# Another table of run lengths for two merged streams, memory of its own for the expert biases' parts, and a wait between head divisions, in a kernel of two transformer layers

## The reference

```
x = x + cross_attention(layernorm(x), ctx, mask)      # 16 heads of 8; 77 context rows, some masked
h = layernorm(x)
y = h + self_attention(layernorm(h) * g1 + c1)        # 16 heads of 8; 512 x 512 scores
z = layernorm(y) * g2 + c2
y = y + expert[argmax(z @ gate_w + gate_b)](z)        # 8 experts: 128 -> 512 (relu) -> 128, each with biases b1, b2
x = x + y
x = x + cross_attention(layernorm(x), ctx)            # scores minus slope * distance
h = layernorm(x)
x = x + h + sigmoid(h @ w_router) * ffn(h) for the 256 tokens of the highest score, x + h for the rest
                                                      # ffn: 128 -> 512 (gelu) -> 128
```

## Time and profile before

| what | value |
|---|---|
| median of three timed runs | 732.77 us (731.79 to 733.81) |
| profiled execution, from first to last instruction | 729.7 us (no time of its own beside the span is given) |
| PE busy | 658.3 us, 90% |
| VectorE busy | 399.1 us, 55% |
| ScalarE busy | 295.5 us, 40% |
| POOL busy | 73.0 us, 10% |
| mean granted clock of PE | 0.963 of 2.4 GHz |

### The profile page before, as it was taken

One profiled execution on the slowest core, in us unless ns is written; L12 is line 12 of the kernel. 1 busy time (PEld: TensorE's weight loads), 2 busy tenths in 40 slices (PEclk: granted clock), 3 DMA queues, 4 the chain that ended last, 5 costly groups with the idle time before them and its releaser, 6 DMA issues.

```text
span 729.7 us, 12018 instructions
## 1 busy us (share of the span) xinstructions
PE 658.3 (90%) x4584; PEld 373.8 (51%) x4588; DVE 399.1 (55%) x924; ACT 295.5 (40%) x354; POOL 73.0 (10%) x82
## 2 busy tenths in 40 slices
PE   3887899999999988899887899999999999999885
PEld 2643434333458645688534453344334388895553
DVE  3635747754852234464716984788348414143657
ACT  1131256356443343242243314645665532314243
POOL 4406401000100001001101100100001000101000
PEclk9997999999999999899998899999999999999998
DMA  8120000000140001310000100000000222200000
GB/s 251 33 91 0 1 1 1 1 1 0 42 129 17 1 2 40 102 45 16 1 1 1 29 1 1 1 1 1 1 1 1 73 73 86 76 2 1 1 1 29
DMA packets 16486, 21.07 MB, mean 29 GB/s; under 512 B 4210, under 2 KB 9419, under 8 KB 16176
## 3 DMA queue, kind: packets, MB, share of 16 engines
q1 hardware_dynamic: 15192, 18.44, 8.2%
q10 hardware_dynamic: 1240, 1.88, 0.8%
HBM read 19.26 MB, written 1.05 MB: 28 GB/s over the span
## 4 chain that ended last, share of the span: by engine, by line
PE 73%; DVE 15%; ACT 5%; issue 3%; POOL 1%; DMA 1%; SPq 0%; POOLq 0%; DVEq 0%
PE pair L908 11%; PE pair L918 8%; PE pair L749 6%; PE pair L970 6%; PE pair L982 6%; PE pair L896 6%; DVE nm L1168 3%; PE pair L855 3%; PE pair L834 3%; PE pair L813 3%; PE pair L946 2%; ACT probs L721 2%; PE pair L809 2%; PE pair L991 2%; PE pair L872 2%
## 5 line engine op out<-in xcount | busy, mean ns | idle before, releaser
L1168 DVE TENSOR_REDUCE nm<-pair 128x2 f32<-128x1024 f32 x128 | 152.5, 1221 | 84.7 <-PE pair L896 84.2
L721 ACT ACTIVATE probs<-pair 128x1024 f32<-128x1024 f32 x128 | 126.7, 1023 | 92.5 <-PE pair L908 46.3
L896 PE MATMUL pair<-k,q 32*128 32x512 f32 x512 | 124.6, 644 | 3.2 <-DVE nm L1168 1.9
L908 PE MATMUL pair<-q,k 32*128 32x512 f32 x512 | 122.1, 629 | 3.1 <-ACT probs L721 2.0
L641 POOL TENSOR_TENSOR rstd<-vareps,small 128x4 f32<-128x4 f32 (+1 forms) x20 | 23.2, 1158 | 591.4 <-DVE vareps L1084 591.3
L908 PEld LDWEIGHTS pair<-q,k 32*128 32x128 f32 x512 | 37.1, 183 | 59.0 <-issue 29.1
L705 ACT ACTIVATE probs<-pair 116x1024 f32<-116x1024 f32 x40 | 39.2, 1022 | 68.5 <-PE pair L855 37.5
L1108 DVE TENSOR_REDUCE nm<-pair 128x6 f32<-128x462 f32 x64 | 37.7, 631 | 47.5 <-PE pair L834 47.5
L918 PE MATMUL pair<-probs,vx 128*32 128x512 f32 x512 | 63.1, 612 | 0.0
L896 PEld LDWEIGHTS pair<-k,q 32*128 32x128 f32 x512 | 37.5, 187 | 22.6 <-issue 7.2
L970 PE MATMUL pair<-zT,w 128*128 (+1 forms) x352 | 48.9, 282 | 0.0
(11 more groups left out here) (172 smaller groups left out, 851.4 us busy)
## 6 DMA issues: line engine op xcount, KB each, us to landing
w<-in_w SPq DMA_DIRECT2D x44, 256.0 KB, 2.8
w<-in_w SPq DMA_DIRECT2D x2, 1024.0 KB
xa<-in_x SPq DMA_DIRECT2D x4, 256.0 KB, 3.2
out_dram<-xc SPq DMA_DIRECT2D x8, 128.0 KB, 1.8
w_sb<-in_w ACTq DMA_DIRECT2D x3, 256.0 KB, 5.1
mask_in<-in_mask SPq DMA_DIRECT2D x4, 154.0 KB, 4.8
wqk<-in_wqk ACTq DMA_DIRECT2D x1, 512.0 KB, 7.0
fw<-in_fw SPq DMA_DIRECT2D x2, 256.0 KB
```

Source lines behind the costliest of these rows:

```text
L721: ins = nc.scalar.activation(dst, src, ACT.Exp)
L896: ins = nc.tensor.matmul(one(q, k), v.q1[rows, g, qt * P:(qt + 1) * P], v.k1[rows, g, :], start=True, stop=True)
L908: ins = nc.tensor.matmul(one(q, k), v.k1[rows, g, kt * P:(kt + 1) * P], v.q1[rows, g, :], start=True, stop=True)
L1168: ins = nc.vector.tensor_reduce(heads[:, 2 * cp:2 * cp + 2, MAXROW:MAXROW + 1], two(q)[:], AX.X, ALU.max, negate=True)
```

## The change

A new table of run lengths puts the same groups of each stream in the same order into another merge, with 287 runs instead of 329. `spare` becomes a buffer of its own, for which the scratch of dynamic DMA is made smaller; ScalarE's wait for the parts is dropped. A `heads1` step on VectorE waits for the preceding one of its batch.

```diff
 TURNS = [
-    4, 1, 1, 2, 3, 4, 2, 1, 6, 1, 1, 1, 5, 1, 2, 1, 4, 1, 5, 1, 5, 1, 5, 1, 2, 4, 1, 2, 2, 1, 1, 1, 1, 2, 4, 1,
...
-    2, 2, 1, 8]
+    2, 2, 1, 1, 2, 4, 2, 1, 8, 4, 1, 1, 2, 1, 2, 1, 3, 1, 1, 2, 2, 2, 1, 2, 4, 1, 2, 1, 11, 1, 12, 1, 4, 1, 2,
...
+    2, 1, 1, 1, 1, 1, 2, 1, 1, 1, 1, 1, 5, 1, 4, 3, 1, 1, 1, 3, 2, 1, 2, 1, 1, 1, 2, 4, 2, 1, 3, 4, 1, 3, 14]
...
-        spare = sets[1].probs.rearrange("p s k n -> p (s k n)")
+        spare = sb("spare", [P, 2048 + 3 * D // 2])
...
                 elif q.kind == "exp":
-                    if b == 1 and x == 0:
-                        act.wait_ge(pool_later, 3)
...
                 elif q.kind == "heads1":
+                    if x:
+                        dve.wait_ge(dve_done[q.p], nth("V", b, "heads1", 1, x - 1))
...
-    nc = bacc.Bacc("TRN2", target_bir_lowering=False, num_devices=1)
+    nc = bacc.Bacc("TRN2", target_bir_lowering=False, num_devices=1, dynamic_dma_scratch_size=2048)
```

## The result

| what | before | changed |
|---|---|---|
| median of four timed runs | 733.14 us (731.79 to 733.81) | 710.70 us (702.37 to 712.06) |
| profiled execution, first to last instruction | 729.7 us | 710.0 us |
| PE busy | 658.3 us | 657.0 us |

The ratio is 0.9664, with a 95% interval of 0.961 to 0.9718: the change makes the kernel 3.4% faster. The forecast of 720 us had the sign, and its range from 712 to 731 us missed the median by 1.3 us. The sizes of its parts were off by more than that, in both directions. The profiles of experiments four and ten are from executions with a long spell of 1.2 GHz near 40 to 60 us that most of their executions don't have; nothing is read from the first, and from the second only rows behind that spell.

The account below looks back on a forecast made before the run. The prediction took PE as the bound, with its waits and 1.2 GHz work to save: 1.4 - 7.9 - 8.2 + 0 + 1.8 = -12.9 us, from 732.77 to about 720 us, range 712 to 731 us.

Parts of the forecast that it names:

- Start: Up to batch 0's first max: PE begins unbroken work about 1.5 us later; +1.4 us, bounds 0 and +3.
- Head: 24.1 to 113.3 us: batch 1's work covers batch 0's wait for z; -7.9 us, bounds -15 and +1.
- run of batch 0's maxima: In the head, 12 steps alone: VectorE 13.6 us against PE's 10, giving 3.3 us of waits.
- Middle: 113.3 to 438.6 us: waits and lost clock fall from 37.1 to 28.9 us; -8.2, bounds -15 and 0.
- hand-over: In the middle, batches 0 and 1 to 2 and 3: 14.0 us, from 10.6 walked, 1.5 short waits, 1.9 added.
- opening of the next self attention: End of the middle: left as it is, 5 of the 19.4 us of the stage to 438.6 us.
- To batch 3's second expert: 438.6 to 655.4 us: same patterns, 5.3 us before and after, change 0.
- Tail: From 655.4 us: batch 2's final sum and output delay batch 3's attention sum; +1.8 us, bounds 0 and +5.
- Edits at nothing: Own memory, dropped ScalarE wait, smaller scratch and head-division wait: worth 0 by themselves; the division wait bounded 0 to 1 us.
- 35 us of ScalarE's stall: New order with the wait kept: ScalarE stands about 35 us at batch 1's first exp until POOL finishes the parts.
- more: Rival: all low-clock spells in head and middle go, only listed waits stay; -23 us, 710 us, chance 0.06.
- Slower: Rival: PE falls to 1.2 GHz in the long runs of one stream; +17 from two runs, 737 us, chance 0.10.

Follow-up runs that it names:

- experiments four: Changed kernel with the old order for the tail, from batch 2's last attention products on; 701.88 us, ratio 0.9557 to the kernel before.
- experiment ten: Changed kernel with batch 1's last exp scores, two products and strips of its first attention moved behind batch 0's z; 718.29 us.
- experiment thirteen: Old table with the change's other edits, POOL's biases' parts moved behind the statistics of batch 1's second norm; 736.88 us, ratio 1.0047 to the kernel before.
- experiment eight: Changed kernel with batch 2's final sum and output moved behind batch 3's score; 710.81 us, against 711.02 for the changed kernel.
- experiment seven: Changed kernel with the old order in the ten groups with batch 3's max steps, keeping the new ranking and feed-forward order; 704.82 us, ratio 0.9614.
- experiment six: Changed kernel with the old tail from batch 3's first exp scores on, keeping the new order of batch 3's max steps; 707.66 us, ratio 0.9603.
- experiment one: Changed kernel with the old table, all other edits kept; 733.98 us against 733.33 for the kernel before, ratio 1.0026.
- experiment eleven: Kernel before with the new table and POOL's biases' parts worked right after its set-up memsets, shared memory and waits kept; 716.13 us, ratio 0.9753.

## Why the prediction was right in sign and wrong in size

The range failed at its lower end because the sum left too many waits in head and middle; the tail, whose loss it named wrongly, gave part of the surplus back.

**Start, +1.4 forecast:** +0.9. Right.

**Head, -7.9 forecast, -15.2 measured: mis-sized.** The mechanism is the one forecast: batch 1's exps between batch 0's sum and its z (experiment ten shows that they are the cover). Two terms of the sum were too large. The waits were put at 9.2 us and are 4.7. Most of the difference is the 3.3 us for the run of batch 0's maxima: I set 13.6 us of VectorE against 10 us of PE, but PE has 12.77 us of work in that run and waits for 0.43 (the first line of the stages above); the projections and v steps between the maxima had been counted too low. VectorE's side was too high as well: ten steps of 1.22 us and a v sum of 0.69 are 12.9 us, and the trace has 11.39. The 3.4 us for spells of 1.2 GHz are 0: I let the two longest waits bring one each, and waits of 1.33, 1.06 and 1.03 us brought none. PE's own work is 0.6 us more than the 68.7 of the sum. The sum has the old wait of 2.96 us for batch 1's maxima gone, rightly, but did not see what it was made of: 1.2 us of it came from POOL's copy, as experiment thirteen shows, and the new order moves that copy of VectorE's to 48 us, ahead of the parts.

**Middle, -8.2 forecast, -13.7 measured: mis-sized.** Waits and lost clock were to come to 28.9 us. Term by term: self attention and routing 5.5, measured 3.4; batch 1's experts 1.0, measured 0.4; hand-over 14.0, measured 10.4. The walk had found 10.6 there, so the 3.4 us beside it (1.5 of short waits and 1.9 for what a walk does not find) were too much. The opening of the next self attention, "which I leave as it is", was 5, and is 0.5. Only the clock was underrated: 3.4, while three spells of 17.1 us in all, with PE busy throughout, cost some 8.5 (half, an estimate). Sum 23.3, 5.6 less than forecast. These terms are read from one profile of each kernel.

**To batch 3's second expert, 0 forecast:** -0.3. Right.

**Tail, +1.8 forecast, +8.6 measured: wrong in its cause.** The step "batch 2's final sum and output ... stand between" failed: experiment eight moves them and changes nothing. What the runs show in its place is two things. Behind batch 3's max steps PE falls to 1.2 GHz, by the times in most executions, and that spell is worth 4.8 us (the two profiles under experiment eight). And batch 3's heads stand behind the ranking on VectorE (the rows there); what that costs by itself experiment seven does not tell from noise. That the waits between the max steps bring the spell is argued, not shown: experiment six has this order and the spell, experiment eight's profile the same waits and no spell. My walk had 1.7 us for a bank at these max steps, where the three waits come to 1.27, and took the tail's clock as unchanged. Of the 8.6 us 7.4 lie ahead of the end of batch 3's sum (707.80 us before, 686.84 with the change), where the forecast had 1.8. Behind it lie only 1.2, in spite of the second spell, so the estimate of 10.0 us above is more than the clock cost in the end.

**Edits at nothing:** right as a sum (experiment one), but the reason given, that the same POOL instructions only write another address, left out that they hold up VectorE, so that their place in time matters. That the new order needs memory of its own is too strong: the parts can be worked early in the shared memory (experiment eleven, 16 us faster than the kernel before), though this early place beside VectorE's copies loses 5 us of the gain by the medians. And the 35 us of ScalarE's stall with the wait kept can't be right by the order itself: POOL comes to the parts only behind batch 0's second norm, which hangs on a step of ScalarE's (the zT of its first attention) that stands behind the waiting exp. Such a program would not go on. This is argued from the order; it was not tried.

**The rivals.** The time came out where the fourth one ("more", 710 us, given 0.06) put it, yet not by its route: head and middle gained 28.9 us, more than its 26.3, and the tail gave nearly 9 back. That its number fits is luck. "Slower" had the fall to 1.2 GHz at the wrong place: not in the long runs (12.77 us busy of 13.20 at clock 1.00, the first line of the stages above) but behind four max steps of the tail, where PE is busy for 4.53 of 5.80 us. What the Trainium skill describes in "TensorE: Matmul & The Clock Gate", section "A second HAM failure mode: psum-queue depth-cycling", a PE that idles briefly between groups of matmuls as it cycles through its PSUM banks and swings between its clock levels, resembles the place in the tail, where PE waits briefly for one bank after the other, and not the runs, which go round their banks as well and stay at 1.00. It does not settle the tail: experiment eight's profile has the same waits there at clock 1.00.

## What to carry to other kernels

A gain that is waits covered by another stream's work is best sized from both sides: in the hand-over the waits of the walk were right in sum within 0.2 us and what was added to them was not there, while in the head one miscount of PE's own work made a wait of 3.3 us out of 0.4. Cut both programs where the same steps are done, and test each piece of a new order by itself: here one piece cost 9 us by the medians, and leaving it out gave 702 us instead of 711. Before work of POOL is called free, look at what VectorE does between SBUF and SBUF beside it.

## What the runs showed of the hardware

An instruction of POOL's holds up VectorE's copies and norms between SBUF and SBUF. Beside a copy of POOL's (8x4096, 3.60 us) VectorE's copies of 128x24 took 3.55 and 1.39 us instead of 0.18, and ended 0.04 and 0.03 us behind it; the four instructions of a norm took 4.78 us instead of 1.10. Beside POOL's casts and subtractions of 0.6 to 1.2 us a norm took 3.34. Reductions that read PSUM do not mind: in the changed kernel twelve of the 128 of the self attention lie beside the parts and take 1220 ns on average, the others 1222. The Trainium skill has this in "SBUF — State Buffer", section "SBUF: two separate sides": VectorE and GpSimd share one pair of ports, and when GpSimd meets a VectorE instruction in a two-port mode (or one with two inputs in SBUF, while GpSimd reads SBUF too), whichever starts first keeps the pair for its whole instruction while the other stands. The traces agree to 0.04 us in the end of the copies; I had not weighed it.

The lower clock is not a fixed cost of an order. By their times and mean clocks, eight of ten executions of the changed kernel had both tail spells and two had not both. Waits of 1.06 and 1.33 us in the head brought no spell. In the tail 13.7 us of it came behind waits of 0.25, 0.71 and 0.31 us in the changed kernel's two profiles, and none behind the same three waits in the profile of experiment eight. What decides between the executions stays open.
